# A gated recurrent layer on one core: joint candidate products in more steps, and results added four steps at a time

## The chip, the cores and the metric

One core of a Trainium2 chip. The metric is the device time of one execution in microseconds; the kernel before takes 1042.9 us (median of 3 runs, 1042.11 to 1043.37). Engines: TensorE (PE, matmuls; PEld is its weight load), VectorE (DVE), ScalarE (ACT) and SyncE (SP, which issues the DMAs). GpSimd (POOL) does nothing here.

## The reference

A GRU with a residual: x has 64 sequences of 128 steps and 512 features, and the result is x plus the states. After every fourth step, except the last, the state is propagated through one more layer before it goes on. All in float32.

```python
x = x + gru(x, cond)              # states of all steps, added to x

def step(h, (x_t, prop)):
    r = sigmoid([x_t, h] @ Wr + br)
    z = sigmoid([x_t, h] @ Wz + bz)
    c = tanh([x_t, r * h] @ Wh + bh)
    h_new = (1 - z) * h + z * c
    h_next = where(prop, tanh(h_new @ Wp + bp), h_new)
    return h_next, h_new          # prop: (t + 1) % 4 == 0 and t < T - 1
```

## The kernel before, in words

The features lie on the 128 partitions in four groups (KC = 4), the 64 sequences in the free dimension, so a state is 128 x 256 values. Steps are taken in blocks of eight (BLOCK = 8, 16 blocks, `m, s = divmod(t, BLOCK)`: s is the place of a step in its block).

Each float32 factor is split in a high and a low float16 part (`h_split`, `q_split`, where q = r * h; `wrec_hi`, `wrec_lo`), and a product with a recurrent matrix is hi·hi + hi·lo + lo·hi. A group of products is 16 matmuls (four by four of 128 x 128 weights). Beside the recurrent part, PE computes the x part of the gates one block ahead for all eight steps at once. For blocks 2 to 14 it uses seven products where eight would be needed (`SEVEN`, `ORDER`, `stage`): 21 stages of 12 matmuls with 256 columns, spread over the eight steps by `STAGES_AT`. ACT begins the quarters of their sums (`begin_quarter`, L551, two copies after most stages), DVE ends some (`end_quarter`, L963), and the last product of a gate waits until the quarter of the sixth is ended (`c22_out`).

PE's order in a step is written out by hand: the products of the reset gate R, of the update gate Z, then of the candidate C with q, then x-part stages; in a step that propagates (s = 3 and 7) stages lie also between C and the products of PROP. Each engine executes its instructions in program order, so a wait holds all that stands behind it.

A group of products is called **joint** where the high weights meet both halves of the state in one matmul with 128 columns (`rec_both`, L1354: 128 x 2 x 64) instead of two with 64 (`rec`, L1346). The two partial sums then lie side by side in PSUM, and DVE adds them with a reduction (L1037 for R, L1055 for Z, L1072 for C) before ACT applies the sigmoid or tanh; ACT seeds both halves with half the x part (L613, 512 values, instead of L622, 256). Joint is Z in every step of `JOINT`, R in those of `JOINT_RESET_AT`, C in those of `JOINT_CANDIDATE_AT`. In a joint reset step four matmuls of the next stage (`AHEAD_OF_C`) stand before the candidate's products, and where the candidate is joint four more (`WITHIN_C`) stand within them.

DVE's order in a step: reductions of R, q in two halves (L1042) and its low part (L1026), reduction of Z, a split of x (L890), reduction of C, `keep` (L1076), `new` (L1096), the new state's high part (L1105), the state itself (L1108), its low part (L1026), the addition of the state to x (L1113), and then at s = 0 the scale of a later block (L849 to L854), sums of x (L950) and quarter updates (L963), as the tables say. When a step propagates, DVE at last makes the next state from ACT's tanh (L1134).

ACT's order: sigmoid of R, splits and squares of x, sigmoid of Z, tanh of C, seeds of R and Z for the next step, the copies of stages, in a propagating step the tanh of PROP ahead of the last ones, and the seed of C. SP stores each half block of x when it is complete (`out_ready`) and then loads the half block four blocks later in its place.

Of the kernel before, what the change touches and what calls it, by code (L numbers as in the profile page):

```python
# [5 lines left out]
ALU = mybir.AluOpType  # L6
# [4 lines left out]
BF16 = mybir.dt.bfloat16  # L11
# [3 lines left out]
P = 128  # L15
CHUNK = 4
BLOCK = 8
RING = 4
R, Z, C, PROP = range(4)
# [15 lines left out]
EARLY_PROP_SHARE = 1.4  # L35
JOINT_RESET_AT = (0, 1, 2, 4, 5, 6)
AHEAD_OF_C = 4
JOINT = range(16, 109)
JOINT_CANDIDATE_AT = (1, 4, 6)
WITHIN_C = 4  # L40
SQUARES_AT = (0, 1, 2, 3)
SCALE_AT = 4
# [27 lines left out]
def gru_kernel(nc, x, h0, wz, wr, wh, wp, biases, out):  # L70
    BLOCKS, _, KC, _, B = x.shape
# [3 lines left out]
    T = BLOCKS * BLOCK  # L75
# [6 lines left out]
    HALF = BLOCK // 2  # L82
# [97 lines left out]
    with ExitStack() as ctx:  # L180
        def sb(name, shape, dt=F32):
            return ctx.enter_context(nc.sbuf_tensor(name, shape, dt))

        def sem(name):
            return ctx.enter_context(nc.semaphore(name))
# [10 lines left out]
        x_blk = [sb(f"x_blk{n}", [P, KC, BLOCK, B]) for n in range(RING)]  # L196
# [63 lines left out]
        LAST_BANKS = (C, C, PROP, PROP)  # L260
        WHOLE = [slice(0, KC)]

        h_even_odd = [sb("h_even", [P, KC, B]), sb("h_odd", [P, KC, B])]
        h_prop = sb("h_prop", [P, KC, B])
        h_split = sb("h_split", [P, KC, 2, B], F16)
        q_split = sb("q_split", [P, KC, 2, B], F16)
# [1 line left out]
        gate = [sb(f"gate{g}", [P, KC, B]) for g in range(4)]  # L268
        q_full = sb("q_full", [P, KC, B])
        keep = sb("keep", [P, KC, B])  # L270
        new = sb("new", [P, KC, B])

        sum_over = sb("sum_over", [P, P], BF16)
        floor = h_even_odd[0][:].rearrange("p k b -> p (k b)").bitcast(BF16)

        squares = gate[PROP][:].rearrange("p k b -> p (k b)").bitcast(BF16)
        early_squares = [x_hi[1][:, 2 * n:2 * n + 2].rearrange("p t n -> p (t n)").bitcast(BF16) for n in range(2)]
# [19 lines left out]
        h_scale, h_unscale = scale[:, HS:HS + 1], unscale[:, HS:HS + 1]  # L297
# [64 lines left out]
        h_new_ready, h_prop_ready = sem("h_new_ready"), sem("h_prop_ready")  # L362
        h_hi_ready, h_lo_ready = sem("h_hi_ready"), sem("h_lo_ready")
        p_hi_ready, p_lo_ready = sem("p_hi_ready"), sem("p_lo_ready")
        out_ready = sem("out_ready")
# [4 lines left out]
        def joint(t):  # L370

            return t in JOINT

        def joint_reset(t):

            return joint(t) and t % BLOCK in JOINT_RESET_AT

        def joint_candidate(t):

            return joint(t) and t % BLOCK in JOINT_CANDIDATE_AT  # L380

# [3 lines left out]
        def candidates_before(t):  # L385
            return sum(joint_candidate(step) for step in range(t))

        def begun(t, n, stages):

            if n != stages[0] or not joint_reset(t):  # L390
                return 0
            return AHEAD_OF_C + (WITHIN_C if joint_candidate(t) else 0)

        def props_before(t):
            return t // CHUNK
# [103 lines left out]
        def _(act):  # L499
# [202 lines left out]
            for t in range(T):  # L702
# [25 lines left out]
                if joint(t):  # L728
                    squash_sums(Z, ACT.Sigmoid, update_summed, JOINT.index(t), WHOLE)
                else:  # L730
# [52 lines left out]
        def _(dve):  # L783
# [244 lines left out]
            for t in range(T):  # L1028
                m, s = divmod(t, BLOCK)
                props = props_before(t)  # L1030
                h_in = h_prop if t % CHUNK == 0 else h_even_odd[(t - 1) % 2]
                h_out = h_even_odd[t % 2]

                if joint_reset(t):
                    dve.wait_ge(product_done[R], t + 1)
# [33 lines left out]
                if joint_candidate(t):  # L1069
                    dve.wait_ge(product_done[C], t + 1)  # L1070
                    for half in HALVES:
# [1 line left out]
                                                ALU.add).then_inc(candidate_summed, 1)  # L1073

                dve.wait_ge(gate_ready[Z], t + 1)
                nc.vector.scalar_tensor_tensor(out=keep[:], in0=gate[Z][:], scalar=-1.0, in1=h_in[:], op0=ALU.add,  # L1076
                                               op1=ALU.mult).then_inc(keep_ready, 1)

                if t == T - 1:
# [4 lines left out]
                                                   op1=ALU.subtract).then_inc(keep_ready, 1)  # L1084
# [9 lines left out]
                for n, half in enumerate(HALVES):  # L1094
                    dve.wait_ge(gate_ready[C], 2 * t + n + 1)
                    nc.vector.scalar_tensor_tensor(out=new[:, half, :], in0=gate[C][:, half, :], scalar=h_scale,  # L1096
                                                   in1=gate[Z][:, half, :], op0=ALU.mult, op1=ALU.mult).then_inc(new_ready, 1)
# [11 lines left out]
                for n, half in enumerate(HALVES):  # L1109
                    dve.wait_ge(hi, count + n + 1)  # L1110
                    dve.wait_ge(h_new_ready, 2 * t + n + 1)
                    subtract_hi(h_out, split, half).then_inc(lo, 1)
                nc.vector.scalar_tensor_tensor(out=x_blk[m % RING][:, :, s, :], in0=h_out[:], scalar=h_unscale,  # L1113
                                               in1=x_blk[m % RING][:, :, s, :], op0=ALU.mult, op1=ALU.add).then_inc(out_ready, 1)
                if m + 2 < BLOCKS and s == scale_at(m + 2):
                    make_x_scale(m + 2)
                wsum_gate, wsum_place = wsum_of(t + 1)
# [27 lines left out]
        def _(pe):  # L1145
# [104 lines left out]
            def stage(m, n, begin=0, stop=PER_GROUP):  # L1250

                g, product = ORDER[n]
                slot_w, slot_x = FACTORS[product]
                bank = bank_of(g, product)
                if begin == 0:
                    wait_stage(m, n)
                for i in range(begin, stop):
                    j, k, part = i // 6, i // 3 % 2, i % 3
                    weights, values = ((win_hi, x_hi), (win_hi, x_lo), (win_lo, x_hi))[part]
                    mm = nc.tensor.matmul(in_halves(x_acc[bank][:])[:, j], weights[g][:, slot_w, k, j * P:(j + 1) * P],  # L1260
                                          in_halves(values[m % 2][:, slot_x, :])[:, k],
                                          start=product in (1, 2) and i == 0, stop=False, skip_group_check=True)
                if stop == PER_GROUP:
                    mm.then_inc(seven_summed, 1)
# [95 lines left out]
            for t in range(T):  # L1360
                m, s = divmod(t, BLOCK)
                first, middle, last = fill_of(t)
                stages_first, stages_last = stages_of(t)
# [58 lines left out]
                if not joint_candidate(t):  # L1422
                    rec(C, wrec_hi, q_split, HIGH, 0, into=into)
                else:
                    stage(m + 1, (stages_first + stages_last)[0], AHEAD_OF_C, AHEAD_OF_C + WITHIN_C)
                if behind:
                    rec(Z, wrec_hi, h_split, HIGH[1:], 1).then_inc(product_done[Z], 1)
                pe.wait_ge(q_lo_ready, 2 * t + 1)
# [67 lines left out]
```

## Time and profile before

| | us |
|---|---|
| median of 3 runs (lowest, highest) | 1042.9 (1042.11, 1043.37) |
| the profiled execution | 1043.28 |
| its span | 1041.3 |
| PE busy, PEld busy | 1034.5, 953.8 |
| DVE busy, ACT busy | 882.1, 776.1 |
| DMA: store of half a block, load of half a block, issue to landing | 3.2, 3.8 |

The page's row of TensorE's granted clock shows the full level (2.4 GHz) in all 40 slices. Busy time of PE is of little use here, since its matmuls are pipelined and their ends are modelled; the starts of successive matmuls tell whether it was kept waiting. DVE and ACT are busy for most of the span too, in stretches without a pause.

### The profile page before, as it was taken

The page shows a single profiled execution, that of the slowest core. Times are in us where ns is not written, and L with a number is a line of the kernel's source. Part 1 is how long each engine was busy: PE and PEld are TensorE (multiplying, and loading weights), DVE is VectorE, ACT ScalarE, POOL GpSimd, SP SyncE. Part 2 cuts the span into 40 slices and gives each one's busy share as a digit, 9 for nine tenths or more (in the row PEclk, how much of TensorE's full clock was granted, in tenths as well). Part 3 has the DMA queues.
Part 4 walks back from the last instruction along what each step waited for, and adds up shares of the span by engine and source line. Part 5 has one row for each costly group of instructions (what it writes and reads, how often), then busy time and mean ns, then how long its engine had stood idle before and what let it go on. Part 6 is the DMA issues. An engine that isn't in the chain of part 4 may idle for free.

```text
span 1041.3 us, 48291 instructions
## 1 busy us (share of the span) xinstructions
PE 1034.5 (99%) x20826; PEld 953.8 (92%) x20826; DVE 882.1 (85%) x2929; ACT 776.1 (75%) x1789; POOL 0.2 (0%) x4
## 2 busy tenths in 40 slices
PE   9999999999999999999999999999999999999998
PEld 4578999999999999999999999999999999999998
DVE  6978888898888998888988888988889988776665
ACT  5877777787777777777777777877777777665565
POOL 0000000000000000000000000000000000000000
PEclk9999999999999999999999999999999999999999
DMA  9312211001111001111011110011110000000001
GB/s 326 114 62 66 83 54 43 31 15 43 43 43 43 22 25 43 43 43 42 5 42 43 43 43 23 23 43 43 43 43 17 30 23 23 23 24 24 24 4 44
DMA packets 38485, 47.27 MB, mean 45 GB/s; under 512 B 2176, under 2 KB 34048, under 8 KB 37888
## 3 DMA queue, kind: packets, MB, share of 16 engines
q1 hardware_dynamic: 38000, 44.12, 12.6%
q8 instruction: 164, 2.69, 1.1%
q14 instruction: 49, 0.40, 0.1%
q10 hardware_dynamic: 272, 0.07, 0.0%
HBM read 27.40 MB, written 16.78 MB: 42 GB/s over the span
## 4 chain that ended last, share of the span: by engine, by line
PE 96%; DVE 2%; DMA 1%; SPq 0%; issue 0%; ACT 0%; DVEq 0%
PE acc L1346 37%; PE x_acc L1260 33%; PE acc L1354 16%; PE x_acc L1150 8%; DMA x_part<-wz_dram 1%; PE x_acc L1281 0%; ACT gate L585 0%; DVE x_lo L890 0%; DVE gate L1037 0%; DVE gate L1055 0%; DVE q_split L1026 0%; DVE q_split L1042 0%; DVE h_split L1105 0%; SPq L415 0%; SPq L412 0%
## 5 line engine op out<-in xcount | busy, mean ns | idle before, releaser
L1260 PE MATMUL x_acc<-x_hi,win_hi 128*128 128x256 f16 x1092 | 297.7, 273 | 0.0
L1260 PE MATMUL x_acc<-x_lo,win_hi 128*128 128x256 f16 x1092 | 297.7, 273 | 0.0
L1260 PE MATMUL x_acc<-x_hi,win_lo 128*128 128x256 f16 x1092 | 297.6, 273 | 0.0
L585 ACT ACTIVATE gate<-gate,unscale 128x128 f32<-128x128 f32 (+1 forms) x303 | 124.2, 434 | 129.0 <-DVE gate L1055 80.5
L591 ACT ACTIVATE gate<-acc,unscale 128x128 f32<-128x128 f32 (+1 forms) x397 | 127.6, 370 | 95.3 <-PE acc L1346 93.5
L1346 PE MATMUL acc<-h_split,wrec_lo 128*128 128x64 f16 x4096 | 180.2, 193 | 0.4 <-DVE h_split L1105 0.4
L1354 PE MATMUL acc<-h_split,wrec_hi 128*128 128x128 f16 x2608 | 172.3, 219 | 0.2 <-DVE h_split L1026 0.2
L551 ACT ACTIVATE x_part<-x_acc,bias,part_unscale 128x256 f32<-128x256 f32 x312 | 154.6, 560 | 17.8 <-PE x_acc L1260 17.7
L1346 PE MATMUL acc<-q_split,wrec_hi 128*128 128x64 f16 x3968 | 160.2, 193 | 0.0
L1346 PEld LDWEIGHTS acc<-h_split,wrec_lo 128*128 128x128 f16 x4096 | 155.0, 98 | 5.5 <-issue 0.6
L1354 PEld LDWEIGHTS acc<-h_split,wrec_hi 128*128 128x128 f16 x2608 | 148.2, 98 | 0.3 <-DVE h_split L1026 0.3
L1346 PEld LDWEIGHTS acc<-q_split,wrec_hi 128*128 128x128 f16 x3968 | 135.1, 98 | 0.0
L613 ACT ACTIVATE acc<-x_part,half_seed_scale 128x512 f32<-128x512 f32 x198 | 130.6, 685 | 0.0
L1346 PE MATMUL acc<-h_split,wrec_hi 128*128 128x64 f16 x2976 | 126.4, 193 | 0.0
L1346 PE MATMUL acc<-q_split,wrec_lo 128*128 128x64 f16 x2544 | 120.5, 193 | 0.4 <-DVE q_split L1042 0.4
L1260 PEld LDWEIGHTS x_acc<-x_hi,win_lo 128*128 128x128 f16 x1092 | 106.8, 98 | 11.2
L1260 PEld LDWEIGHTS x_acc<-x_hi,win_hi 128*128 128x128 f16 x1092 | 106.8, 98 | 10.6
L1260 PEld LDWEIGHTS x_acc<-x_lo,win_hi 128*128 128x128 f16 x1092 | 106.8, 98 | 10.1
L1346 PEld LDWEIGHTS acc<-q_split,wrec_lo 128*128 128x128 f16 x2544 | 98.5, 98 | 6.2 <-issue 1.1
L1346 PEld LDWEIGHTS acc<-h_split,wrec_hi 128*128 128x128 f16 x2976 | 103.5, 98 | 0.0
L622 ACT ACTIVATE acc<-x_part,seed_scale 128x256 f32<-128x256 f32 x185 | 85.5, 477 | 1.8
L1096 DVE SCALAR_TENSOR_TENSOR new<-gate,scale 128x128 f32<-128x128 f32 x254 | 77.5, 348 | 0.9 <-ACT gate L591 0.9
(147 smaller groups left out, 1508.3 us busy)
## 6 DMA issues: line engine op xcount, KB each, us to landing
out_dram<-x_blk SPq DMA_DIRECT2D x30, 512.0 KB, 3.2
x_blk<-x_dram SPq DMA_DIRECT2D x24, 512.0 KB, 3.8
x_blk<-x_dram SPq DMA_DIRECT2D x3, 1024.0 KB, 9.2
x_part<-wz_dram SPq DMA_DIRECT2D x4, 256.0 KB, 7.2
x_part<-wh_dram SPq DMA_DIRECT2D x4, 256.0 KB, 7.0
x_part<-wr_dram SPq DMA_DIRECT2D x1, 1024.0 KB, 11.4
x_part<-wz_dram SPq DMA_DIRECT2D x1, 1024.0 KB, 13.6
x_part<-wh_dram SPq DMA_DIRECT2D x1, 1024.0 KB, 17.3
```

The costliest lines, as they stand in the source:

```text
L551: nc.scalar.activation(part_quarter(m, g, jh, nh)[:, j], in_halves(x_acc[bank][:])[:, j], ACT.Identity, bias=bias[:, g, 2 * jh + j:2 * jh ...
L585: nc.scalar.activation(gate[g][:, half], gate[g][:, half], func, scale=unscale[:, g:g + 1]).then_inc(gate_ready[g], 1)
L591: nc.scalar.activation(gate[g][:, half, :], acc[g][:, half, :], func, scale=unscale[:, g:g + 1]).then_inc(gate_ready[g], 1)
L613: nc.scalar.activation(acc_bank[g][:], added.unsqueeze(1).broadcast_to([P, 2, KC, B]), ACT.Copy, scale=half_seed_scale[:, g:g + 1]).then_i ...
L622: nc.scalar.activation(acc[g], added, ACT.Copy, scale=seed_scale[:, g:g + 1]).then_inc(seed_ready[g], 1)
L1096: nc.vector.scalar_tensor_tensor(out=new[:, half, :], in0=gate[C][:, half, :], scalar=h_scale, in1=gate[Z][:, half, :], op0=ALU.mult, op1= ...
L1150: return nc.tensor.matmul(x_acc[bank][:, 0:cols], weights[g][:, 2 * (j // 2) + k // 2, k % 2, j % 2 * P:(j % 2 + 1) * P], values[m % 2][:, ...
L1260: mm = nc.tensor.matmul(in_halves(x_acc[bank][:])[:, j], weights[g][:, slot_w, k, j * P:(j + 1) * P], in_halves(values[m % 2][:, slot_x, : ...
L1346: mm = nc.tensor.matmul(bank[:, j, :], weights[g][:, k, j * P:(j + 1) * P], values[:, k, lo, :], start=False, stop=False, skip_group_check ...
L1354: mm = nc.tensor.matmul(acc_bank[g][:, :, j, :], wrec_hi[g][:, k, j * P:(j + 1) * P], values[:, k], start=False, stop=False, skip_group_ch ...
```

## The change

Three things are changed. The candidate's products are joint also at s = 3 and s = 7, the steps that propagate (`JOINT_CANDIDATE_AT`); there no stage matmuls stand ahead of C, but four within (`ahead_of_candidate`). The joint form begins at step 19 instead of 16. And the states are kept in a ring of eight (`h_ring`); they are added to x four steps at a time, at steps with t % 4 == 0 for the four steps before (`results_at`), from step 124 on also one by one. The larger ring makes the kernel ask for less scratch memory for DMA descriptors.

```diff
-JOINT = range(16, 109)
-JOINT_CANDIDATE_AT = (1, 4, 6)
+JOINT = range(19, 109)
+JOINT_CANDIDATE_AT = (1, 3, 4, 6, 7)
...
-        h_even_odd = [sb("h_even", [P, KC, B]), sb("h_odd", [P, KC, B])]
+        h_ring = sb("h_ring", [P, KC, BLOCK, B])
...
+        def ahead_of_candidate(t):
+
+            return AHEAD_OF_C if joint_reset(t) else 0
+
         def begun(t, n, stages):
 
-            if n != stages[0] or not joint_reset(t):
-                return 0
-            return AHEAD_OF_C + (WITHIN_C if joint_candidate(t) else 0)
+            return ahead_of_candidate(t) + (WITHIN_C if joint_candidate(t) else 0) if n == stages[0] else 0
+
+        def results_at(t):
+
+            if t >= T - CHUNK:
+                return [range(t - CHUNK, t), range(t, t + 1)] if t % CHUNK == 0 else [range(t, t + 1)]
+            return [range(t - CHUNK, t)] if t and t % CHUNK == 0 else []
...
-                h_in = h_prop if t % CHUNK == 0 else h_even_odd[(t - 1) % 2]
-                h_out = h_even_odd[t % 2]
+                h_in = h_prop[:] if t % CHUNK == 0 else h_ring[:, :, (t - 1) % BLOCK]
+                h_out = h_ring[:, :, t % BLOCK]
...
-                nc.vector.scalar_tensor_tensor(out=x_blk[m % RING][:, :, s, :], in0=h_out[:], scalar=h_unscale,
-                                               in1=x_blk[m % RING][:, :, s, :], op0=ALU.mult, op1=ALU.add).then_inc(out_ready, 1)
+                for steps in results_at(t):
+                    results = x_blk[steps.start // BLOCK % RING][:, :, steps.start % BLOCK:steps.start % BLOCK + len(steps)]
+                    states = h_ring[:, :, steps.start % BLOCK:steps.start % BLOCK + len(steps)]
+                    if steps[-1] == t:
+                        dve.wait_ge(h_new_ready, 2 * t + 2)
+                    nc.vector.scalar_tensor_tensor(out=results, in0=states, scalar=h_unscale, in1=results, op0=ALU.mult,
+                                                   op1=ALU.add).then_inc(out_ready, len(steps))
...
-                    stage(m + 1, (stages_first + stages_last)[0], AHEAD_OF_C, AHEAD_OF_C + WITHIN_C)
+                    stage(m + 1, (stages_first + stages_last)[0], ahead_of_candidate(t), ahead_of_candidate(t) + WITHIN_C)
...
-    nc = bacc.Bacc("TRN2", target_bir_lowering=False, num_devices=1)
+    nc = bacc.Bacc("TRN2", target_bir_lowering=False, num_devices=1, dynamic_dma_scratch_size=8192)
```

On DVE, at the end of a step with s = 0 and the beginning of the next one, this stands before (acc and gate are here those of the scale's sum and of R; L1113 is the add to x):

```order
L1113 SCALAR_TENSOR_TENSOR x_blk<-h_even,unscale,x_blk 128x4x64
L849 TENSOR_REDUCE square_sum<-acc 128x1
L804 TENSOR_SCALAR root<-square_sum 128x1
L807 TENSOR_SCALAR x_pow<-root 128x1
L809 TENSOR_SCALAR x_scale<-x_pow 128x1
L854 TENSOR_SCALAR part_unscale<-unscale,x_pow 128x3
L1037 TENSOR_REDUCE gate<-acc 128x128 x2
L1042 TENSOR_TENSOR q_split<-gate,h_even 128x2x64 x2
```

And now, with L1126 as the add:

```order
L1126 SCALAR_TENSOR_TENSOR x_blk<-h_ring,unscale,x_blk 128x4x256
L857 TENSOR_REDUCE square_sum<-acc 128x1
L812 TENSOR_SCALAR root<-square_sum 128x1
L815 TENSOR_SCALAR x_pow<-root 128x1
L817 TENSOR_SCALAR x_scale<-x_pow 128x1
L862 TENSOR_SCALAR part_unscale<-unscale,x_pow 128x3
L1045 TENSOR_REDUCE gate<-acc 128x128 x2
L1050 TENSOR_TENSOR q_split<-gate,h_ring 128x2x64 x2
```

The add stands at the same place and is four times as large; in the three steps before it there is none.

On PE, the candidate's products in a step that propagates (s = 3) and the x-part matmuls behind them, before:

```order
L1346 MATMUL acc<-q_split,wrec_lo 128x64 x8
L1346 MATMUL acc<-q_split,wrec_hi 128x64 x8
L1346 MATMUL acc<-q_split,wrec_lo 128x64 x8
L1346 MATMUL acc<-q_split,wrec_hi 128x64 x24
L1260 MATMUL x_acc<-x_hi,win_hi 128x256
L1260 MATMUL x_acc<-x_lo,win_hi 128x256
```

And now:

```order
L1359 MATMUL acc<-q_split,wrec_lo 128x64 x16
L1273 MATMUL x_acc<-x_hi,win_hi 128x256
L1273 MATMUL x_acc<-x_lo,win_hi 128x256
L1273 MATMUL x_acc<-x_hi,win_lo 128x256
L1273 MATMUL x_acc<-x_hi,win_hi 128x256
L1367 MATMUL acc<-q_split,wrec_hi 128x2x64 x16
L1273 MATMUL x_acc<-x_lo,win_hi 128x256
```

32 narrow matmuls with the high weights have become 16 wide ones, and four x-part matmuls have moved from behind the candidate's products to between them; 20 stay behind.

## Rows read from the trace of the kernel before

**Rows 1.** The page: the span and the chain that ended last, by engine.

```profile
span 1041.3 us, 48291 instructions
...
PE 96%; DVE 2%; DMA 1%; SPq 0%; issue 0%; ACT 0%; DVEq 0%
```

**Rows 2.** Three stretches: limits and length, then each engine's busy time and instruction count.

```profile
616.99:680.26 63.27, 63.27 (x1232) 60.12 (x1229) 56.60 (x189) 48.93 (x112) 0.00 (x0) 1.00 0.11 36
172.28:195.33 23.05, 22.11 (x408) 20.38 (x406) 21.03 (x71) 17.37 (x38) 0.00 (x0) 1.00 0.10 35
616.99:638.50 21.51, 21.51 (x407) 20.43 (x405) 19.74 (x69) 16.14 (x36) 0.00 (x0) 1.00 0.12 38
```

**Rows 3.** Timeline of PE in steps 76 and 77: start, length, engine, line, operation, count.

```profile
656.00 0.86 PE L1346 MATMUL acc<-h_split,wrec_lo 128*128 128x64 f16 x24
656.70 1.06 PE L1354 MATMUL acc<-h_split,wrec_hi 128*128 128x128 f16 x16
657.60 0.40 PE L1346 MATMUL acc<-h_split,wrec_lo 128*128 128x64 f16 x8
...
659.18 0.39 PE L1346 MATMUL acc<-q_split,wrec_lo 128*128 128x64 f16 x8
```

**Rows 4.** Timeline of DVE, end of step 76 and start of step 77.

```profile
656.14 0.48 DVE L1113 SCALAR_TENSOR_TENSOR x_blk<-h_even,unscale,x_blk 128x256 f32<-128x256 f32 x1
656.54 1.41 DVE L963 SCALAR_TENSOR_TENSOR x_part<-x_acc,part_unscale,x_part 128x512 f32<-128x512 f32 x2
657.86 0.75 DVE L1037 TENSOR_REDUCE gate<-acc 128x128 f32<-128x256 f32 x2
658.74 0.62 DVE L1042 TENSOR_TENSOR q_split<-gate,h_even 128x128 f16<-128x128 f32 x2
```

**Rows 5.** Timeline of DVE, end of step 80 and start of step 81.

```profile
687.64 0.48 DVE L1113 SCALAR_TENSOR_TENSOR x_blk<-h_even,unscale,x_blk 128x256 f32<-128x256 f32 x1
...
688.82 0.76 DVE L1037 TENSOR_REDUCE gate<-acc 128x128 f32<-128x256 f32 x2
```

**Rows 6.** Timeline of PE in step 81.

```profile
690.18 0.63 PE L1346 MATMUL acc<-q_split,wrec_lo 128*128 128x64 f16 x16
```

**Rows 7.** Groups of instructions by line and shape: count, busy us, mean ns, idle before.

```profile
L1113 DVE SCALAR_TENSOR_TENSOR x_blk<-h_even,unscale,x_blk 128x256 f32<-128x256 f32 x64 | 30.9, 483 | 0.0
...
L883 DVE SCALAR_TENSOR_TENSOR x_lo<-x_blk,x_scale,x_hi 128x1024 f16<-128x1024 f32 x2 | 2.5, 1278 | 0.0
```

**Rows 8.** Timeline of ACT in step 75, a propagating step.

```profile
643.65 1.30 ACT L613 ACTIVATE acc<-x_part,half_seed_scale 128x512 f32<-128x512 f32 x2
644.87 1.93 ACT L551 ACTIVATE x_part<-x_acc,bias,part_unscale 128x256 f32<-128x256 f32 x4
646.94 0.63 ACT L591 ACTIVATE gate<-acc,unscale 128x128 f32<-128x128 f32 x2
```

**Rows 9.** Timeline of PE and DVE at the end of step 75.

```profile
645.28 0.40 PE L1346 MATMUL acc<-q_split,wrec_lo 128*128 128x64 f16 x8
...
647.99 0.86 PE L1346 MATMUL acc<-h_split,wrec_lo 128*128 128x64 f16 x24
...
647.34 0.54 DVE L1134 TENSOR_SCALAR h_split<-gate,scale 128x128 f16<-128x128 f32 x2 [0.91 <-ACT gate L591]
```

**Rows 10.** Timeline of DVE and ACT in step 76, whose candidate is joint.

```profile
653.28 0.75 DVE L1072 TENSOR_REDUCE gate<-acc 128x128 f32<-128x256 f32 x2
...
654.81 0.61 DVE L1105 TENSOR_TENSOR h_split<-new,keep 128x128 f16<-128x128 f32 x2
...
655.74 0.49 DVE L1026 TENSOR_TENSOR h_split<-h_even,h_split 128x128 f16<-128x128 f32 x2
...
654.38 1.28 ACT L613 ACTIVATE acc<-x_part,half_seed_scale 128x512 f32<-128x512 f32 x2
```

**Rows 11.** Timeline of DVE and PE in step 79, a propagating step.

```profile
678.01 0.74 DVE L963 SCALAR_TENSOR_TENSOR x_part<-x_acc,part_unscale,x_part 128x512 f32<-128x512 f32 x1
...
678.95 0.27 PE L1260 MATMUL x_acc<-x_hi,win_hi 128*128 128x256 f16 x1
```

More of the change, by code:

```diff
@@ L273, in gru_kernel @@
         sum_over = sb("sum_over", [P, P], BF16)
-        floor = h_even_odd[0][:].rearrange("p k b -> p (k b)").bitcast(BF16)
+        floor = h_ring[:, 0, 0:HALF].rearrange("p s b -> p (s b)").bitcast(BF16)
         squares = gate[PROP][:].rearrange("p k b -> p (k b)").bitcast(BF16)
@@ L1075, in _ @@
                 dve.wait_ge(gate_ready[Z], t + 1)
-                nc.vector.scalar_tensor_tensor(out=keep[:], in0=gate[Z][:], scalar=-1.0, in1=h_in[:], op0=ALU.add,
+                nc.vector.scalar_tensor_tensor(out=keep[:], in0=gate[Z][:], scalar=-1.0, in1=h_in, op0=ALU.add,
                                                op1=ALU.mult).then_inc(keep_ready, 1)
```

## The prediction

> **What bounds the kernel now.** I read the page first. The chain that ended last is 96% TensorE [rows 1], but a busy PE says little, since ends of matmuls are modelled. So the second view is a timeline of PE, read by starts: a matmul with 64 columns follows the last one after 0.029 us (24 of them from 656.00 to 656.70), one with 128 columns after 0.056 us (16 from 656.70 to 657.60) [rows 3]. 24 matmuls with 256 columns fill 645.28 − 2.62 = 642.66 to 645.28, where the propagation's products begin [rows 9]; that is 0.109 us each. With these three prices the block of eight steps from 616.99 to 680.26 [rows 2] is full: PE is never kept waiting there. Whatever delays a product by more than its own slack is lost for good, and whatever takes work from DVE or ACT without such a wait gains nothing. The reader is to look for slack, not for busy shares.
>
> The third view is the DVE timeline where a joint reset step begins. In step 77 PE would reach the reset-gated product at 657.60 + 8 × 0.029 + 16 × 0.056 + 4 × 0.109 = 659.17, and starts it at 659.18 [rows 3]. The first of the two q halves starts at 658.74 and takes 0.29 of the pair's 0.62 [rows 4]; it ends at 659.03, and 0.15 later PE starts. So the slack is zero there. The reduction ahead of it (657.86) begins where the two quarter updates before it end, 656.54 + 1.41 − 0.09 [rows 4]: DVE works without a pause from the add to x at 656.14 up to this reduction. In step 81 the same: reduction at 688.82, q half ready 0.88 + 0.29 later at 689.99, with 0.15 on top 690.14, and PE starts at 690.18 [rows 5, 6]; slack 0.04.
>
> **The add four steps at a time.** It removes 127 adds of 0.483 us and brings 31 of 1024 elements. The same operation on 1024 elements takes 1.278 us [rows 7]. DVE has 0.64 us less work in four steps, but all that is left falls in one step, t = 0 modulo 4, ahead of the updates or the scale chain and the next step's reduction, where DVE had no pause. The add grows by 1.28 − 0.48 = 0.80 us. Queued behind it are the reductions of the reset gate, for them waits ACT's sigmoid, for that DVE's q, and for q PE.
> - Steps 21, 29 ... 101 (11 of them, as step 77): 0.80 − 0 = 0.80 us each, 8.8 us.
> - Steps 25, 33 ... 105 (11, as step 81): 0.80 − 0.04 = 0.76, taken as 0.77 for the second half of q, 8.5 us.
> - Steps 5, 9, 17 and 109 are not joint in their reset gate (17 by this change), but have lumps of DVE work too. Each can lose 0 to 0.80; where DVE runs without a pause into q it loses nearly all. I take 0.7 each, 2.7 us. In step 13 and in the last four blocks of four I take nothing: DVE waits for the gate there, and the lump fits.
> In the other three steps of four DVE gains 0.40 us, which PE cannot use: its slack is already positive there. Bounds of the term: 0 if DVE had hidden slack, and 26 × 0.80 = 20.8 us. The rows leave no such slack, so I take 8.8 + 8.5 + 2.7 = 20.0 us.
>
> A rule of the Trainium skill speaks for the change here: VectorE: DVE Perf Modes, "The TRN2 errata", says that each SBUF-source instruction pays a fixed extra, so that one large tile is cheaper than many small ones. This trace agrees on the size (four adds 1.93 us, one large 1.28). By that rule alone DVE would be done sooner in each four steps, and the sum would lose its first term: 1049.3 us, or 1040.6 if nothing else waits either (the rival Faster). Rows 4 and 5 speak against it: what counts there is when the large one runs.
>
> **The candidate joint beside propagations** (23 steps: 19, 27 ... 107 and 23, 31 ... 103). On PE, 32 narrow matmuls become 16 wide: 32 × 0.029 = 0.93 against 16 × 0.056 = 0.89, so 0.04 us saved. Joint products are lost in steps 16 to 18 (7 groups). Net 16 × 0.04 = 0.6 us gained. That is all that PE gains, since a wide matmul costs as much as two narrow ones.
>
> The Trainium skill (TensorE: Matmul & The Clock Gate, "Back-to-back issue gap") gives a sustained 81 ns for pairs of weight load and matmul at 128 columns. Here they follow after 56 ns; the measurement decides. By the rule a wide group would be 16 × 0.081 − 0.93 = 0.37 us longer than the narrow ones, not 0.04 shorter, and 16 net groups would make the sum 6.5 us larger.
>
> The chain gets longer. Four of the 24 x-part matmuls move in between the candidate's products, so these end at 642.66 + 4 × 0.109 − 0.04 = 643.06 in step 75, and the cover before the propagation's products is 20 × 0.109 = 2.18 us. DVE then reduces before ACT's tanh. The reduction can start some 0.21 after the last issue (657.86 against 657.60 is 0.26 with DVE late), at 643.27. In step 76, where this form is at work, the first half of the new state starts 654.81 − 653.28 = 1.53 after the reduction and takes 0.29 [rows 10]. Thus the propagation's input is there at 643.27 + 1.82 = 645.09, plus 0.15 is 645.24, and PE comes at 643.06 + 2.18 = 645.24. Just hidden; 0 to 0.2 us each, I take 0. But two other things are queued behind:
> - Step 75's kind (12): ACT. After the tanhs come two seeds, four x-part copies, then the propagation's tanh [rows 8]. In joint form the seeds start 654.38 − 653.28 = 1.10 after the reduction [rows 10], at 644.37 and not 643.65 (+0.72). The copies then start at 645.59, run 1.93, less 0.09 of overlap, and the propagation's tanh starts at 647.43 instead of 646.94: +0.49, ACT's pause ahead of it being used up. PE starts the next step at 647.99 [rows 9], or at 647.95 with the 0.04 saved. Its input comes (647.34 − 646.94) + 0.29 + 0.15 = 0.84 after that tanh's start [rows 8, 9], at 648.27. Wait 0.32, and 0.05 more for the low half. Between 0 and 0.5; I take 0.37, in all 4.4 us.
> - Step 79's kind (11): DVE. Its quarter update (678.01) must end before PE's last seven-product group (678.95) may begin [rows 11]. Here the candidate's reduction starts at 675.54 by the same sum, and the low half of p ends 655.74 + 0.49 − 653.28 = 2.95 later [rows 10], at 678.49. The update starts at 678.41, although the add is gone, ends at 679.15, and PE starts at 679.30 instead of 678.91. Wait 0.39; bounds 0 and 0.5; in all 4.3 us.
>
> **Joint from step 19.** Steps 16 to 18 last 23.05 us where the same three steps of a later block last 21.51 [rows 2]. The 1.54 us are waits of PE for DVE, whose joint reductions collide there with the extra splits and sums of two blocks. Without them 1.5 us come back (bounds 0 and 1.5), of which the lump at step 17 has been counted above. Another 0.2 us of small waits behind single adds go.
>
> **The rest.** Ring addressing costs nothing: the operations keep element counts. Stores start one step later, and with them the loads that they release on SP's queue; a block is read two steps and more after its load is due, so this stays hidden, and costs at most one step's time once if it did not. The scratch size touches no queue that is used.
>
> **The sum.** 20.0 + 4.4 + 4.3 − 0.6 − 1.5 − 0.2 = 26.4 us. The profiled execution took 1043.28 us, 1.98 beyond its span of 1041.3; with the change 1069.7. The median of before is 1042.9, 0.4 lower; so 1069.3. A steady block of 63.27 us becomes 63.27 + 0.80 + 0.77 + 0.37 + 0.39 − 0.08 = 65.5.
>
> **Rivals.**
> - Only the lump costs: ACT's copies or the update at step 79 find an earlier start than I give them, and the joint candidate is hidden. For it: the propagation's own input is just in time. Against: both waits come out of sums of queued work without a pause. 1069.3 − 8.7 = 1060.6.
> - Only the joint candidate costs, the lump is hidden (for instance the add on a faster path than 1.04 ns an element). For it: nothing in the trace but that it never shows this very form. Against: 256, 1024 elements lie on one line [rows 7]. 1069.3 − 20.0 = 1049.3.
> - Faster: PE is bound by its matmuls, DVE's lump meets slack that the trace doesn't show, and the step-16 waits go. The place is the reset-gated product in steps 77 and 81; this is decided by whether the reduction starts before about 657.9 and 688.8 on the old clock. Then −0.6 − 1.5 − 0.2, 1040.6. Against: zero slack in both places.
> - Worse: the propagation's input, with no slack left, is late by 0.2 to 0.4 us in all 23 steps: 1069.3 + 7 = 1076.
>
> **Chances.** My forecast 0.66, its own range 1064 to 1074. Only the lump 0.17, only the candidate 0.05, faster 0.05, worse 0.07. The range for 8 in 10 takes in the lump alone and half of the worse case: 1057 to 1076. About 0.2%, or 2 us, is what a measurement here can tell from no change. Faster 0.05, within it 0.02, slower 0.93.
>
> **What would show it.** In the profile after: the large add at 1.28 us; a wait of PE of some 0.8 us ahead of the first q product in steps 5 and 1 of each block, released by DVE; ACT's copies running into the propagation's tanh without a pause in step 3 of a block and PE waiting 0.3 there; the last x-part group of step 7 late by 0.4; steady blocks of 65.5 us; steps 16 to 18 without their long waits. A steady block near 63.2 would prove the lump wrong, one near 64.8 the candidate's part.

## The result and the profile after

The kernel after takes 1067.24 us (median of 4 runs, 1066.41 to 1067.86), the kernel before on the same chip 1042.51 (4 runs, 1042.0 to 1043.37). The ratio is 1.0237, with a 95% interval of 1.0225 to 1.025. The profiled execution took 1067.86 us, its span is 24.8 us longer than before [rows 1]. The first rows of the page are the span and the busy time of each engine:

```profile
span 1066.1 us, 47737 instructions
...
PE 1042.3 (98%) x20570; PEld 952.7 (89%) x20570; DVE 880.3 (83%) x2871; ACT 782.7 (73%) x1789; POOL 0.2 (0%) x4
```

DVE does slightly less than before and the kernel is slower: the sum of the work says nothing here. Two stretches, the block of eight steps from 632.96 to 698.11 (steps 72 to 79, the same steps as the block of [rows 2]) and steps 16 to 18, in the form of [rows 2]:

```profile
632.96:698.11 65.15, 63.93 (x1200) 59.95 (x1198) 57.10 (x187) 49.63 (x112) 0.00 (x0) 1.00 0.11 35
176.91:198.71 21.80, 21.80 (x519) 20.83 (x517) 17.91 (x64) 16.21 (x38) 0.00 (x0) 1.00 0.16 51
```

The block has grown by 1.88 us, from 63.27. Steps 16 to 18 have shrunk from 23.05 to 21.80. The groups of instructions by line have the large add, with its count, busy time, mean of one in ns and idle time before:

```profile
L1126 DVE SCALAR_TENSOR_TENSOR x_blk<-h_ring,unscale,x_blk 128x1024 f32<-128x1024 f32 x31 | 39.7, 1282 | 0.2
```

**Step 77, where the add meets the reset gate.** DVE's timeline (start, length, engine, line, operation, count):

```profile
673.05 1.28 DVE L1126 SCALAR_TENSOR_TENSOR x_blk<-h_ring,unscale,x_blk 128x1024 f32<-128x1024 f32 x1
674.25 1.41 DVE L971 SCALAR_TENSOR_TENSOR x_part<-x_acc,part_unscale,x_part 128x512 f32<-128x512 f32 x2
675.57 0.75 DVE L1045 TENSOR_REDUCE gate<-acc 128x128 f32<-128x256 f32 x2
676.46 0.63 DVE L1050 TENSOR_TENSOR q_split<-gate,h_ring 128x128 f16<-128x128 f32 x2
```

and PE's, with the idle time before an instruction and its releaser in brackets:

```profile
676.08 0.27 PE L1273 MATMUL x_acc<-x_hi,win_hi 128*128 128x256 f16 x1
676.89 0.39 PE L1359 MATMUL acc<-q_split,wrec_lo 128*128 128x64 f16 x8 [0.54 <-DVE q_split L1050]
```

This is the chain of [rows 3, 4] with a longer first link. The last x-part matmul ahead of the candidate starts at 676.08 and would be followed after 0.109; q's product starts at 676.89. PE loses 0.70 us (the brackets give less, since they count from a modelled end). In step 81 it is the same, q's product being late by 0.75 [rows 6]:

```profile
708.76 0.40 PE L1359 MATMUL acc<-q_split,wrec_lo 128*128 128x64 f16 x8 [0.57 <-DVE q_split L1050]
```

**Step 75, whose candidate is now joint.** ACT's timeline, and the first product of step 76 on PE, to be held against [rows 8, 9]:

```profile
661.10 1.28 ACT L621 ACTIVATE acc<-x_part,half_seed_scale 128x512 f32<-128x512 f32 x2
662.32 1.91 ACT L559 ACTIVATE x_part<-x_acc,bias,part_unscale 128x256 f32<-128x256 f32 x4
664.12 0.63 ACT L599 ACTIVATE gate<-acc,unscale 128x128 f32<-128x128 f32 x2
```

```profile
664.58 0.27 PE L1273 MATMUL x_acc<-x_hi,win_lo 128*128 128x256 f16 x1
664.95 0.42 PE L1359 MATMUL acc<-h_split,wrec_lo 128*128 128x64 f16 x9
```

The four copies now run without a pause into the propagation's tanh. PE starts step 76 at 664.95 instead of 664.58 + 0.109 = 664.69: 0.26 late, and 0.07 more before the low half of the new state's products.

**Step 79.** The end of DVE's chain, and PE's last x-part group [rows 11]:

```profile
693.25 0.75 DVE L1080 TENSOR_REDUCE gate<-acc 128x128 f32<-128x256 f32 x2
...
695.99 0.74 DVE L971 SCALAR_TENSOR_TENSOR x_part<-x_acc,part_unscale,x_part 128x512 f32<-128x512 f32 x1
```

```profile
696.33 0.46 PE L1359 MATMUL acc<-q_split,wrec_hi 128*128 128x64 f16 x10
696.79 0.28 PE L1273 MATMUL x_acc<-x_hi,win_hi 128*128 128x256 f16 x1
```

Ten narrow matmuls from 696.33 end their turn at 696.62; the next starts at 696.79. The wait is 0.17, in ten of the eleven such steps, and 0.52 in step 39.

**The first blocks, which the prediction passed over.** SP's queue after, the times being those at which a DMA is issued (a store of half a block of results, a load of half a block of x, a load of weights for the seven-product sums):

```profile
84.77 0.62 SPq L474 DMA_DIRECT2D out_dram<-x_blk  x1
89.69 0.63 SPq L479 DMA_DIRECT2D x_blk<-x_dram  x1
90.36 0.62 SPq L463 DMA_DIRECT2D sum_c<-wr_dram  x1
```

The same three before:

```profile
75.40 0.63 SPq L466 DMA_DIRECT2D out_dram<-x_blk  x1
79.42 0.63 SPq L471 DMA_DIRECT2D x_blk<-x_dram  x1
86.25 0.38 SPq L455 DMA_DIRECT2D sum_c<-wr_dram  x1
```

The store waits for the add of four steps and comes 9.4 us later. The load waits for the store to have landed. Behind both stands the load of weights, which before was issued 6.8 us after the load of x, once DVE had freed its buffer, and now comes right behind it. It is 4.1 us later than before, and DVE and then PE wait for it in step 6:

```profile
94.40 0.69 DVE L927 TENSOR_TENSOR sum_c<-sum_c,sum_b 128x512 f32<-128x512 f32 x1 [3.09 <-DMA sum_c<-wr_dram]
```

```profile
96.05 0.39 PE L1359 MATMUL acc<-q_split,wrec_lo 128*128 128x64 f16 x8 [1.83 <-DVE q_split L1050]
```

The list of waits (engine and line, releaser; us in total, times, longest) has the two that follow in steps 10 and 14 as well:

```profile
DVE sum_c L927 <- DMA sum_c<-wr_dram: 3.1, 1, 3.1
...
DVE sum_c L927 <- DMA sum_c<-wz_dram: 2.3, 1, 2.3
...
DVE sum_c L927 <- DMA sum_c<-wh_dram: 2.2, 1, 2.2
```

A wait of PE is here what the distance between the starts of two matmuls has over the 0.029, 0.056 or 0.109 us of [rows 3, 9]. Added up step by step, the whole difference is this:

| where | difference, us |
|---|---|
| up to the start of step 0, where PE waits for the first loads | −0.92 |
| steps 0 to 15: steps 5 and 9 1.5, steps 6, 10 and 14 4.1 | +5.56 |
| steps 16 to 18 | −1.52 |
| steps 19 to 107 | +21.34 |
| steps 108 to 127 | +1.0 |
| closer matmuls (16 wide groups more) | −0.64 |
| sum; the spans differ by 24.8 | +24.8 |

### The profile page after: what moved, and what is told of

It is laid out like the page before. It is cut to its first block, busy times and chain, and to the rows that moved or that the text cites. A ratio compares the mean times of both kernels' runs of the same rounds, so it can differ in the third digit from the quotient of the medians.

```text
span 1066.1 us, 47737 instructions
## 1 busy us (share of the span) xinstructions
PE 1042.3 (98%) x20570; PEld 952.7 (89%) x20570; DVE 880.3 (83%) x2871; ACT 782.7 (73%) x1789; POOL 0.2 (0%) x4
## 4 chain that ended last, share of the span: by engine, by line
PE 78%; DVE 15%; ACT 3%; DMA 2%; issue 2%; SPq 0%; DVEq 0%; ACTq 0%
PE acc L1359 30%; PE x_acc L1273 27%; PE acc L1367 13%; PE x_acc L1163 7%; DVE x_blk L1126 2%; ACT gate L593 2%; DVE x_part L971 2%; PE x_acc L1294 1%; DVE q_split L1050 1%; DVE gate L1045 1%; DMA out_dram<-x_blk 1%; DVE gate L1063 1%; DVE h_split L1113 1%; DVE q_split L1034 1%; DVE h_split L1034 1%
## 5 line engine op out<-in xcount | busy, mean ns | idle before, releaser
L593 ACT ACTIVATE gate<-gate,unscale 128x128 f32<-128x128 f32 (+1 forms) x338 | 136.6, 430 | 154.5 <-DVE gate L1063 78.3
L599 ACT ACTIVATE gate<-acc,unscale 128x128 f32<-128x128 f32 (+1 forms) x362 | 117.5, 373 | 87.8 <-PE acc L1359 87.7
L1367 PE MATMUL acc<-h_split,wrec_hi 128*128 128x128 f16 x2512 | 166.2, 220 | 0.0
L621 ACT ACTIVATE acc<-x_part,half_seed_scale 128x512 f32<-128x512 f32 x214 | 141.7, 683 | 0.0
L1359 PE MATMUL acc<-h_split,wrec_hi 128*128 128x64 f16 x3168 | 134.6, 194 | 0.0
L1359 PE MATMUL acc<-q_split,wrec_lo 128*128 128x64 f16 x2544 | 117.2, 193 | 17.7 <-DVE q_split L1050 17.5
L1359 PE MATMUL acc<-q_split,wrec_hi 128*128 128x64 f16 x3264 | 133.2, 194 | 0.0
L1359 PEld LDWEIGHTS acc<-q_split,wrec_hi 128*128 128x128 f16 x3264 | 111.9, 98 | 0.1
L1050 DVE TENSOR_TENSOR q_split<-gate,h_ring 128x128 f16<-128x128 f32 x192 | 53.9, 292 | 43.5 <-ACT gate L599 35.7
L630 ACT ACTIVATE acc<-x_part,seed_scale 128x256 f32<-128x256 f32 x169 | 77.6, 477 | 1.8
```

Of the source, the lines that this page charges most:

```text
L593: nc.scalar.activation(gate[g][:, half], gate[g][:, half], func, scale=unscale[:, g:g + 1]).then_inc(gate_ready[g], 1)
L599: nc.scalar.activation(gate[g][:, half, :], acc[g][:, half, :], func, scale=unscale[:, g:g + 1]).then_inc(gate_ready[g], 1)
L621: nc.scalar.activation(acc_bank[g][:], added.unsqueeze(1).broadcast_to([P, 2, KC, B]), ACT.Copy, scale=half_seed_scale[:, g:g + 1]).then_i ...
L630: nc.scalar.activation(acc[g], added, ACT.Copy, scale=seed_scale[:, g:g + 1]).then_inc(seed_ready[g], 1)
L1050: nc.vector.tensor_tensor(q_split[:, half, 0, :], gate[R][:, half, :], h_in[:, half, :], ALU.mult).then_inc(q_hi_ready, 1)
L1359: mm = nc.tensor.matmul(bank[:, j, :], weights[g][:, k, j * P:(j + 1) * P], values[:, k, lo, :], start=False, stop=False, skip_group_check ...
```

## The experiments

Each is told by its difference from one of the two kernels. All are compared with the kernel before on the same chip.

**j19: the joint form from step 19, alone.** The kernel before with one line changed.

```diff
-JOINT = range(16, 109)
+JOINT = range(19, 109)
```

> The kernel before with the joint form from step 19 alone. Theory A (PE waits in steps 16 to 18 for crowded joint reductions on DVE): those waits of 1.5 us go, seven groups cost 0.04 us more each, so 1.2 us faster than before, about 1041.3 us, and no wait of PE in steps 16 to 18. Rival B (the waits come from the splits and sums themselves, joint or not): they stay, and the time is 0.3 us longer than before, 1042.8.

Measured: 1041.94 us (11 runs) against 1042.64 (21 runs); ratio 0.9996, 0.9987 to 1.0004. PE waits 0.00 us in steps 16 to 18, so in the trace the 1.5 us are gone. The span is 1039.9, that is 1.4 shorter, but this agrees by chance: step 0 starts 1.0 us earlier in this trace (46.5 against 47.5), the 1.5 come on top, and 0.9 of new waits behind short pauses of DVE (see the last section) and 0.3 for the seven groups are lost again. In the medians 0.7 us are left, which can't be told from nothing.

**j19_four: the lump without the joint candidate.** The kernel after with the candidate as before.

```diff
-JOINT_CANDIDATE_AT = (1, 3, 4, 6, 7)
+JOINT_CANDIDATE_AT = (1, 4, 6)
```

> The changed kernel with the candidate joint only where it was before (s = 1, 4, 6): joint from 19 and the add of four steps. Theory A (the lump of 1.28 us sits in front of the reset reductions, and SP's queue is late in the first blocks): 7.7 us in steps 5 of the blocks, 7.5 in steps 1, 1.0 at step 109 and 5.5 in the first 16 steps, over 1041.3, so 1063. Rival B (the joint candidate is the main cost, as by a shifted chain in all steps): close to 1044.

Measured: 1063.24 us (4 runs); ratio 1.0197, 1.0183 to 1.0211. Waits 0.75 us at s = 1 and 0.70 at s = 5, 5.67 us in the first 16 steps, 0.88 at step 109, none at s = 3, 4 and 7. The add alone costs 21.3 us over j19.

**cand: the joint candidate without the lump.** The kernel after with the ring, but the add in each step.

```diff
-            if t >= T - CHUNK:
-                return [range(t - CHUNK, t), range(t, t + 1)] if t % CHUNK == 0 else [range(t, t + 1)]
-            return [range(t - CHUNK, t)] if t and t % CHUNK == 0 else []
+            return [range(t, t + 1)]
```

> The changed kernel with the adds one step at a time again, with ring, joint from 19 and joint candidates at s = 3 and 7. Theory A: 12 x 0.33 us for ACT's queue at s = 3, and 11 x 0.57 at s = 7, since the single add comes back in front of the quarter update (0.17 + 0.40), less 0.9 for the wide groups, over 1041.3: 1050.7. Rival B (lump and candidate need each other; alone the candidate is hidden, as the propagation's input is just in time): 1040.5.

Measured: 1051.23 us (4 runs); ratio 1.0082, 1.0069 to 1.0096. Waits 0.26 at s = 3, 0.07 at s = 4 and 0.57 at s = 7. That last one is 0.17 in the kernel after, 0.40 less, since DVE's add of 0.48 (0.40 after overlap) is gone from the chain there. DVE at the end of step 79:

```profile
682.16 0.47 DVE L1124 SCALAR_TENSOR_TENSOR x_blk<-h_ring,unscale,x_blk 128x256 f32<-128x256 f32 x1
682.56 0.74 DVE L969 SCALAR_TENSOR_TENSOR x_part<-x_acc,part_unscale,x_part 128x512 f32<-128x512 f32 x1
```

```profile
683.36 0.28 PE L1271 MATMUL x_acc<-x_hi,win_hi 128*128 128x256 f16 x1 [0.40 <-DVE x_part L969]
```

So the parts do not add up. The add costs 21.3 us over j19 and the candidate 9.3, together 30.6; the kernel after costs 25.3. Of the 5.3 between, 11 × 0.40 = 4.4 are this place, where the large add takes work away from the path that the joint candidate puts there. The first 16 steps are at 0.26 us of waits, as before: the ring and the smaller scratch memory alone are free, and the 4.1 us on SP's queue belong to the late add.

**cand7 and cand_act: the two mechanisms of the candidate apart.** cand7 makes it joint at s = 7 only; cand_act keeps both and lets ACT do the last stage's two copies behind the propagation's tanh at s = 3.

```diff
-JOINT_CANDIDATE_AT = (1, 3, 4, 6, 7)
+JOINT_CANDIDATE_AT = (1, 4, 6, 7)
```

```diff
+                    late_copies = stages_first[-1:] if s == 3 else ()
                     for n in stages_first:
-                        read_stage(m + 1, n)
+                        if n not in late_copies:
+                            read_stage(m + 1, n)
...
                     squash(PROP, ACT.Tanh, props_before(t), HALVES)
+                    for n in late_copies:
+                        read_stage(m + 1, n)
```

> As the run with single adds and joint candidates, but the candidate joint at s = 7 only, not at s = 3. Theory A (two separate queues): 11 x 0.57 less 0.4, over 1041.3, 1047.2; no wait of PE at the start of steps 4. Rival B (one effect, the longer chain before the propagation's products): half of the loss of the run with both.

> As the run with single adds and joint candidates, with one change on ACT: at s = 3 the two copies of the later stage stand behind the propagation's tanh instead of ahead of it. Theory A (four copies hold up that tanh by 0.3 us net): PE's waits at the start of steps 4 go, 4.0 us less than that run, about 1046.7. Rival B (the tanh is late because the propagation's products are late): no difference, 1050.7.

Measured: cand7 1048.11 us (4 runs; 1.0049, 1.0034 to 1.0064), 0.57 at s = 7 and nothing at s = 3 and 4. cand_act 1047.6 us (4 runs; 1.0049, 1.0032 to 1.0066), again nothing at s = 3 and 4, although the candidate is joint there; 0.57 at s = 7 stays. ACT in its step 75:

```profile
647.34 1.00 ACT L557 ACTIVATE x_part<-x_acc,bias,part_unscale 128x256 f32<-128x256 f32 x2
648.65 0.62 ACT L597 ACTIVATE gate<-acc,unscale 128x128 f32<-128x128 f32 x2 [0.32 <-PE acc L1361]
649.17 1.02 ACT L557 ACTIVATE x_part<-x_acc,bias,part_unscale 128x256 f32<-128x256 f32 x2
```

The tanh now waits 0.32 us for PE, and not for the copies. This shows two things: the wait at s = 3 is ACT's order, and the joint candidate's own chain is hidden, for with the copies out of the way nothing is late. "Worse" falls with it. It is hidden with next to nothing to spare, as the prediction's sum had it: in step 63 of cand a pause of 0.28 us in DVE's part of that chain makes PE start the propagation's products 553.22 − 552.84 − 0.109 = 0.27 late.

```profile
552.84 0.27 PE L1271 MATMUL x_acc<-x_hi,win_lo 128*128 128x256 f16 x1
553.22 0.39 PE L1357 MATMUL acc<-q_split,wrec_lo 128*128 128x64 f16 x8
```

**j19_two: two steps at a time.** j19_four with a smaller lump, twice as often.

```diff
-                return [range(t - CHUNK, t), range(t, t + 1)] if t % CHUNK == 0 else [range(t, t + 1)]
-            return [range(t - CHUNK, t)] if t and t % CHUNK == 0 else []
+                return [range(t - 2, t), range(t, t + 1)] if t % CHUNK == 0 else [range(t, t + 1)]
+            return [range(t - 2, t)] if t and t % 2 == 0 else []
```

> As the run with four steps' adds and the candidate as before, but two steps at a time: a lump of 0.75 us where the single add took 0.48, so 0.27 more. Theory A (what passes the slack of 0.04 and 0.10 us is lost): 10 x 0.23 and 11 x 0.17 in steps 1 and 5, 4 us for the quarter loads, 0.6 elsewhere, over 1041.3: 1050. Rival B (loss in proportion to the added size of the operation, 0.27 of 0.80): 1041.3 + 0.34 x 21.7 = 1048.7 with the waits at steps 6, 10 and 14 a third of 4.1 us each in sum.

Measured: 1048.6 us (4 runs); ratio 1.0057, 1.0042 to 1.0072. DVE at the start of step 77 and PE at q's product:

```profile
660.49 0.75 DVE L1126 SCALAR_TENSOR_TENSOR x_blk<-h_ring,unscale,x_blk 128x512 f32<-128x512 f32 x1
661.16 1.41 DVE L971 SCALAR_TENSOR_TENSOR x_part<-x_acc,part_unscale,x_part 128x512 f32<-128x512 f32 x2
662.48 0.75 DVE L1045 TENSOR_REDUCE gate<-acc 128x128 f32<-128x256 f32 x2
```

```profile
663.52 0.27 PE L1273 MATMUL x_acc<-x_hi,win_hi 128*128 128x256 f16 x1
663.80 0.39 PE L1359 MATMUL acc<-q_split,wrec_lo 128*128 128x64 f16 x8
```

The wait is 663.80 − 663.52 − 0.109 = 0.17 at s = 5, and 0.22 at s = 1. An add of 512 elements takes 0.27 us more than one of 256, one of 1024 takes 0.80 more. Slack is the time by which an input is ready before PE comes to it. Both sizes give the same: 0.27 − 0.17 and 0.80 − 0.70 are 0.10 at s = 5, 0.27 − 0.22 and 0.80 − 0.75 are 0.05 at s = 1. The cost is the lump's growth less this slack. The other half of the small lumps, at t = 2 modulo 4, brings no wait at s = 3 and 7 beyond 0.1 us in two steps. The median lies on the number of rival B (1048.7) and not on that of theory A (1050), but the waits decide for A: B's share of a third would be about 0.25 at both places and 1.4 us in steps 6, 10 and 14, where 3.0 are measured.

**moved: the same large add, elsewhere.** The candidate as before; the add of the four steps stands at the end of the propagating step, behind its sums and quarter updates, where DVE would wait for ACT's tanh.

```diff
             if t >= T - CHUNK:
-                return [range(t - CHUNK, t), range(t, t + 1)] if t % CHUNK == 0 else [range(t, t + 1)]
-            return [range(t - CHUNK, t)] if t and t % CHUNK == 0 else []
+                return [range(t, t + 1)]
+            return [range(t - CHUNK + 1, t + 1)] if t % CHUNK == CHUNK - 1 else []
...
-                for steps in results_at(t):
...
                 if m + 2 < BLOCKS and s == scale_at(m + 2):
                     make_x_scale(m + 2)
...
+                for steps in results_at(t):
...
                 if prop:
```

> Joint from 19, candidate as before, and the add of four steps moved to the end of the propagating step itself, behind the sums and quarter updates, where DVE waits 0.85 to 0.91 us for ACT's tanh in the kernel before. Theory A (place, not size, of the lump matters): freed of the single add DVE has 1.25 us there and the lump needs 1.20, so no wait; the stores are in time too, since a half block is complete at the same step as before; 1040.6 us, a little faster than before. Rival B (a large add is slow wherever it stands, by contention or a slower access pattern): some 20 us slower, 1060.

Measured: 1041.26 us (11 runs, 1040.04 to 1041.71) against 1042.64; ratio 0.9984, 0.9975 to 0.9993. 22 us faster than j19_four with the same 31 large adds (1277 ns). DVE at the end of step 75, and the block that answers to [rows 2]:

```profile
643.53 0.69 DVE L958 TENSOR_TENSOR sum_b<-x_blk,sum_b 128x512 f32<-128x512 f32 x1
644.13 1.28 DVE L1142 SCALAR_TENSOR_TENSOR x_blk<-h_ring,unscale,x_blk 128x1024 f32<-128x1024 f32 x1
645.53 0.55 DVE L1147 TENSOR_SCALAR h_split<-gate,scale 128x128 f16<-128x128 f32 x2
```

```profile
615.17:678.43 63.26, 63.26 (x1232) 60.12 (x1230) 55.83 (x183) 48.93 (x112) 0.00 (x0) 1.00 0.11 36
```

Before, DVE waits 0.91 us there for the tanh [rows 9]; with 0.40 of the single add gone the gap is 1.31, and the large add fits in. From step 19 to 107 PE waits 0.14 us in all, in steps 56 and 57. The first 16 steps have 0.31 us of waits, none of them for a load of weights. It is the fastest kernel of this study, faster than before by 0.16%; it can't be told from j19.

**after_sp: the queue's order.** The kernel after, with the loads of weights ahead of the stores and loads of half blocks in blocks 0 and 1.

```diff
             for m in range(LAST):
-                store(m, FIRST)
-                if m + RING < BLOCKS:
-                    load_half(m + RING, FIRST)
+                if m > 1:
+                    store(m, FIRST)
                 if m == 0:
                     load_sums_last(R)
...
-                store(m, SECOND)
+                if m <= 1:
+                    store(m, FIRST)
                 if m + RING < BLOCKS:
-                    load_half(m + RING, SECOND)
+                    load_half(m + RING, FIRST)
+                if m:
+                    store(m, SECOND)
                 if m == 0:
...
+                    store(m, SECOND)
+                if m + RING < BLOCKS:
+                    load_half(m + RING, SECOND)
```

> The changed kernel with SP's order altered in the first two blocks: the loads of weight quarters for the sums stand ahead of the stores and loads of half blocks. Theory A (DVE's weight sums wait for quarter loads that stand in SP's queue behind a store's completion, which is a step later now): waits of PE of 2.0, 0.8 and 1.3 us in steps 6, 10 and 14 go, so 4.1 us less than the changed kernel, 1063.1. Rival B (these waits come from the lump on DVE alone): no difference, 1067.2.

Measured: 1065.34 us (4 runs); ratio 1.0217, 1.0202 to 1.0232. The waits in steps 6, 10 and 14 are gone, all 4.1 us; those of 0.67 and 1.03 in steps 5 and 9 stay. But step 11 now waits 1.23 us. A half block of x is issued at 133.26 behind its store, the median of these loads lands 3.6 us after its issue, and ACT's squares, which read x, start at 136.86. That they wait for this load is read from these times; the view names no releaser.

```profile
136.86 0.63 ACT L656 ACTIVATE gate<-x_blk 128x512 bf16<-128x512 f32 x1 [2.32 <-issue]
```

Step 0 starts 0.8 us later than in the kernel after; in the traces of the eleven kernels step 0 starts between 46.3 and 47.5, so this belongs to no edit. 4.1 − 1.2 − 0.8 = 2.1 is what the spans differ by (2.0). The cause is shown; the repair is not free, and the expectation missed the load.

**moved_narrow: what the joint form is worth.** moved with no joint step.

```diff
-JOINT = range(19, 109)
+JOINT = range(200, 201)
```

> The kernel with the add moved into the propagating step, and no joint product at all: 191 groups (67 of R, 90 of Z, 34 of C) go back from 16 matmuls with 128 columns to 32 with 64. Theory A (PE's starts: 0.029 us for a narrow and 0.056 for a wide one): 191 x 0.039 = 7.4 us more than that kernel, 1048.7, since the slack of DVE only grows. Rival B (weight loads set PE's pace, so that a narrow matmul costs as much as a wide one): 191 x 16 x 0.056 = 171 us more.

Measured: 1051.35 us (4 runs) against 1042.61; ratio 1.0087, 1.007 to 1.0104. Steps 19 to 108, in moved and in moved_narrow (length, then busy time and count by engine):

```profile
193.76:907.21 713.45, 713.45 (x13866) 677.96 (x13864) 624.54 (x2038) 548.96 (x1259) 0.00 (x0) 1.00 0.11 35
```

```profile
193.88:916.50 722.62, 721.79 (x16922) 689.00 (x16919) 508.26 (x1751) 506.72 (x1259) 0.00 (x0) 1.00 0.11 35
```

9.2 us, of which 191 groups × 0.039 = 7.4 are the spacing of the matmuls. 1.5 are waits of 0.48 to 0.54 us in steps 36, 40 and 76, and 0.3 small ones. In step 36 the wait lies between two matmuls of one group, while ACT waits for PE and DVE for ACT; what PE waits for there stays open. The expected 1048.7 had no such waits and was 2.7 us too low. 3056 matmuls less bring 0.039 us for each 16 of them, and cost DVE 116 us and ACT 42 of extra work, which is what makes the slack so small in this kernel. The Trainium skill's figure of 81 ns for a sustained pair at 128 columns (TensorE: Matmul & The Clock Gate, "Back-to-back issue gap") would have made the narrow form faster by 191 × 0.37 = 71 us, an estimate; the runs decide for 55.9 ns.

## Why the prediction was right, and where it was not

The forecast of 1069.3 us was 2.1 too high, with the direction and both mechanisms right. The steady block was close, 65.5 against 65.15, though that is 2.25 us of growth against 1.88. By its own steps:

- **Step 5 of a block**, 11 × 0.80 = 8.8: measured 0.70 each (one 0.84), 7.8. The slack there is 0.10, as j19_two and j19_four both show. I had read it from step 77 alone, and there the pair at L1105 took 0.61 [rows 10] and not the 0.49 that it takes in nearly all other steps of that trace (its halves start 0.32 apart there, 0.20 elsewhere). One block was taken for eleven, and it was the odd one: the slow pair holds one of the pauses of DVE told in the last section. The wait of 0.84, in step 69, has such a pause too.
- **Step 1 of a block**, 11 × 0.77 = 8.5: 0.75 each at ten steps, 7.5. Step 105 has no scale chain, DVE waits 0.68 us there before, and it loses nothing: a miscount.
- **Steps 5, 9, 17 and 109**, 2.7: 0.67, 0.80, 0 and 0.93 over before, 2.4.
- **s = 3**, 12 × 0.37 = 4.4: 0.26 and 0.07, 4.0. cand_act shows ACT's order as the cause.
- **s = 7**, 11 × 0.39 = 4.3: 0.17 each, 1.9, and 0.35 once. The place and the releaser were right, two prices not. From the reduction to the update I took 2.87 us, with the slow pair of [rows 10] in it; it is 695.99 − 693.25 = 2.74. And PE starts 0.06 after the update's end (696.73, 696.79), not 0.15.
- **Work and steps 16 to 18**, −0.6 and −1.5: −0.64 and −1.52. The small waits, −0.2: the 0.26 us that step 25 had before are now part of its 0.75, 0.17 in steps 34, 43 and 94 are gone, and 0.10 in step 82 is new.
- **The adds**: 124 go and 31 come, not 127 and 31, since the last are still added one by one. No term hangs on it.
- **"A block is read two steps and more after its load is due, so this stays hidden"** is the step that failed. It looked at who reads the block that is loaded. The loads of weights behind it in the same queue are wanted at once; they cost 4.1 us in steps 6, 10 and 14, in three places and not "once". after_sp takes exactly these waits away.

The rows sum to 7.8 + 7.5 + 2.4 + 4.0 + 1.9 + 4.1 − 0.64 − 1.52 = 25.5, and with 0.92 us from the start 24.6 of the 24.8. So a part of the closeness is luck: a term of 4.1 us that was not seen stands against 5.1 us that the seen ones were too dear and 0.9 us of the start.

Of the rivals, "only the lump costs" (1060.6) falls by the waits at s = 3 and s = 7 in cand and after; "only the candidate" and "faster" by j19_four. That the sizes of the add lie on one line was said from two points, which always do; j19_two has the third, 0.746 us for 512 elements where the line gives 0.748. The rule that one large tile is cheaper than four small ones (the Trainium skill, VectorE: DVE Perf Modes, "The TRN2 errata") holds in its size, 1.28 us against 4 × 0.48. Its place decides the rest: at t % 4 == 0 it cost some 21 us, at the end of the propagating step nothing.

## What to carry to other kernels

Where an engine with an ordered queue feeds a full one, work gathered into a larger instruction costs its growth less the slack at the place where it lands; put it into a gap that the trace shows to be larger, and read that gap in several repetitions, not in one. When a result comes later, follow every transfer behind its store in the same queue, not only the buffer that the store frees. A saving on an engine that waits anyway is no gain, but it can pay for another change at the same place.

## What the runs showed of the hardware

- Where PE waits for a half of q or h after x-part matmuls, 0.15 us lie between DVE's end and PE's start ([rows 3, 4]: 659.03 to 659.18); for a quarter update it is 0.06 (696.73 to 696.79).
- A matmul of 128 columns, 0.056 us, replaces two of 64 at 0.029, each with its own weights loaded. Loading weights half as often saves nearly nothing: 0.039 us in 16 matmuls.
- DVE pauses now and then for 0.1 to 0.3 us between two of its own instructions that otherwise follow without a gap, where it has no other engine to wait for. In step 63 of cand one such pause (0.19 and the lost overlap of 0.09, 0.28) makes PE's wait 0.85 us in place of 0.57; where there is slack PE does not see it. The places are not left to chance. cand_act, whose DVE instructions are those of cand, has the pause at the same instruction:

```profile
551.98 0.60 DVE L1102 SCALAR_TENSOR_TENSOR new<-gate,scale 128x128 f32<-128x128 f32 x2
552.78 0.49 DVE L1111 TENSOR_TENSOR q_split<-new,keep 128x128 f16<-128x128 f32 x2 [0.19 <-DVE new L1102]
```

```profile
551.12 0.49 DVE L1115 TENSOR_TENSOR q_split<-new,keep 128x128 f16<-128x128 f32 x2 [0.19 <-DVE new L1106]
```

- So it is with all twelve such pauses of cand and cand_act, and with all ten of after and after_sp. Numbered from 0 in the trace's order, the records of DVE's sequencer included, the eight pauses of the kernel before stand at DVE's records 575, 831, 1088, 1343, 2367, 2880, 3391 and 3519, each 63 or 64 above a multiple of 128; those of after and cand are placed likewise. The one at 2367 is the slow pair of [rows 10]. Why they come there is not shown. But a change that adds or removes instructions on DVE moves them to other steps, and so moves some tenths of a microsecond between two traces.
